# TensorE's block loop of a mixture of experts: 16 blocks a turn in place of four

## The reference

```python
T = x.shape[0]
scores = jax.nn.sigmoid(x @ gate_w)
...
_, selected_experts = jax.lax.top_k(masked_scores, K)
...
g = jax.lax.ragged_dot(xs, w_gate, group_sizes)
u = jax.lax.ragged_dot(xs, w_up, group_sizes)
d = jax.lax.ragged_dot(jax.nn.silu(g) * u, w_down, group_sizes)
...
expert_out = jnp.sum(out * weights[..., None], axis=1)
```

## Time and profile before

| what | us |
| --- | --- |
| median of 3 runs (lowest, highest) | 2470.41 (2468.43, 2471.7) |
| the profiled execution | 2471.61 |
| its span, first to last instruction | 2469.9 |
| PE busy | 2253.3 (91%) |
| PEld busy | 1931.8 (78%) |
| POOL busy | 1444.7 (58%) |
| DVE busy | 1266.8 (51%) |
| ACT busy | 1165.3 (47%) |

### The profile page before, as it was taken

One profiled execution on the slowest core, in us unless ns is written; L12 is line 12 of the kernel. 1 busy time (PEld: TensorE's weight loads), 2 busy tenths in 40 slices (PEclk: granted clock), 3 DMA queues, 4 the chain that ended last, 5 costly groups with the idle time before them and its releaser, 6 DMA issues. The chain is left out here.

```text
span 2469.9 us, 42008 instructions
## 1 busy us (share of the span) xinstructions
PE 2253.3 (91%) x12059; PEld 1931.8 (78%) x12060; DVE 1266.8 (51%) x2118; ACT 1165.3 (47%) x2503; POOL 1444.7 (58%) x980
## 2 busy tenths in 40 slices
PE   2899999999999999898989899999999799999776
PEld 1678888888888877776778699999988699999654
DVE  8767777777766656758643322222222122222365
ACT  4467777777777767776621123333332133333210
POOL 7877777777755558566713144441579956430376
PEclk9999999999999999999979999999999899999988
DMA  4533444443354456453357144442557655442476
GB/s 116 162 95 111 123 129 158 149 129 120 119 184 143 132 179 200 142 172 108 130 204 283 46 138 158 137 156 88 170 171 228 195 170 182 149 168 76 122 206 183
DMA packets 285670, 372.37 MB, mean 151 GB/s; under 512 B 20212, under 2 KB 187192, under 8 KB 280824
## 3 DMA queue, kind: packets, MB, share of 16 engines
q1 hardware_dynamic: 231224, 252.46, 32.7%
q10 hardware_dynamic: 38976, 68.17, 8.4%
q0 software_dynamic: 15360, 50.34, 6.2%
HBM read 257.66 MB, written 113.25 MB: 150 GB/s over the span
## 5 line engine op out<-in xcount | busy, mean ns | idle before, releaser
L1925 POOL TENSOR_SCALAR we_high<-we_raw 128x1408 fp32r<-128x1408 f32 (+1 forms) x95 | 134.0, 1410 | 396.5 <-PE up_e L650 315.9
L1927 POOL TENSOR_TENSOR we_low<-we_raw,we_high 128x1408 fp32r<-128x1408 f32 (+1 forms) x95 | 314.5, 3311 | 7.9
L2056 DVE TENSOR_TENSOR hT_low<-hT_ps,hT_high 128x256 fp32r<-128x256 f32 x127 | 54.0, 425 | 391.5 <-ACT hT_high L2019 391.5
L2069 DVE TENSOR_TENSOR hidden_e<-silu_e,up_e 128x352 f32<-128x352 f32 x127 | 66.2, 521 | 283.5 <-ACT silu_e L2030 283.5
L2030 ACT ACTIVATE silu_e<-gate_e 128x352 f32<-128x352 f32 x127 | 59.0, 465 | 316.7 <-PE up_e L650 316.7
L650 PE MATMUL gate_e<-we_high,xT_high 128*128 x508 | 177.7, 350 | 20.8 <-POOL we_low L1927 20.4
L2035 ACT ACTIVATE rows_out<-down_e 128x512 f32<-128x512 f32 x127 | 75.9, 598 | 215.5 <-PE down_e L650 215.5
L650 PE MATMUL gate_e<-we_high,xT_low 128*128 x508 | 166.0, 327 | 0.0
L650 PE MATMUL gate_e<-we_low,xT_high 128*128 x508 | 165.7, 326 | 0.0
L650 PE MATMUL up_e<-we_high,xT_high 128*128 x508 | 164.4, 324 | 0.0
L650 PE MATMUL up_e<-we_low,xT_high 128*128 x508 | 163.1, 321 | 0.0
(11 more groups left out here) (341 smaller groups left out, 7341.8 us busy)
## 6 DMA issues: line engine op xcount, KB each, us to landing
rows_early<-slots_in ACTq DMA_DIRECT2D x129, 256.0 KB, 2.7
slots_out<-rows_out ACTq DMA_DIRECT2D x127, 256.0 KB, 2.0
we_raw<-L_ffn_w_gate SPq DMA_DIRECT2D x32, 704.0 KB, 4.4
we_raw<-L_ffn_w_up SPq DMA_DIRECT2D x32, 704.0 KB, 5.0
w_ring<-L_attn_Wq SPq DMA_DIRECT2D x64, 256.0 KB, 3.2
q_T<-q_out SPq DMA_DIRECT2D x64, 256.0 KB, 2.5
w_ring<-L_attn_Wk SPq DMA_DIRECT2D x64, 256.0 KB, 3.5
w_ring<-L_attn_Wv SPq DMA_DIRECT2D x64, 256.0 KB, 3.9
```

The lines of the kernel that those rows point to most:

```text
L1925: nc.gpsimd.tensor_scalar(wh[:, p, at:to], raw[:, at:to], 1.0, 1.0, ALU.mult, ALU.mult).then_inc(w_hi, 1)
L1927: nc.gpsimd.tensor_tensor(wl[:, p, at:to], raw[:, at:to], wh[:, p, at:to].bitcast(F32), ALU.subtract).then_inc(w_split, 1)
L2069: nc.vector.tensor_tensor(hb[:], sg[:], psu[:], ALU.mult).then_inc(h_done, 1)
```

## The change

One argument differs: TensorE's loop holds 16 steps. By `pipeline`, steps 0 to 15 are written out, steps 16 to 111 are six turns of the loop, and steps 112 to 128 (17 of them) are written out. The other four engines' streams have the same instructions in the same order.

```diff
-            pipeline(pe, NBLK, 4, 2, step)
+            pipeline(pe, NBLK, 16, 2, step)
```

## The result

The changed kernel is slower. Its median of 4 runs is 2492.24 us (2490.94 to 2495.31), against 2469.52 of the kernel before in the runs beside it (2468.43 to 2471.70): a ratio of 1.0093, with 1.0075 to 1.0110 as its 95% interval. Forecast were 2478.1 with 2460 to 2487 as the range, so the sign of the likeliest case was right and the time lies outside the range. The profiled execution took 2493.31, which is 14.0 more than the 2479.3 forecast for it.

What follows compares the result with a forecast made beforehand. TensorE's steps were taken as the bound, with the sequencer's branch and late even steps on top, except where GpSimd bounds. Returns costing 16.4 less 8.7 saved gave 7.7 us longer: 2478.1 us, range 2460 to 2487.

Steps and rivals of the forecast that it cites:

- the likeliest case: TensorE's loop code comes back by packets at each return, so the kernel is 7.7 us longer; chance 0.68.
- the mechanism and the places: The loop's nine pages are not held; the array idles 2 to 4 us ahead of steps 32, 48, 64, 80, 96.
- The written-out stretches: Steps 3 to 15 and 112 to 123, written out at 6.67 us each, save 1.9 and 1.3 us.
- the one behind 63: The return behind step 63 costs 4.1 us, swallowed by TensorE's wait for GpSimd of 7.26 us.
- the wait at 1931: TensorE's wait for `we_low`, 7.26 us before, grows if the steps ahead of it get shorter.
- the price of a return, 4.1 us: At the loop's branch back: 2.65 us of idle array plus slow clock, 4.1; four returns count, 16.4 us.
- The upper end in the text: Highest cost of the loop's returns: 4 x (4.4 + 1.7), about 24 us.
- The fetch, 2.4 us: Bringing back a page of code at a return takes 2.4 us, between data landings of 2.0 and 2.7.
- The clock, 1.7 us: Behind a return the array's clock is at 0.50 for 3.4 us, costing half of that, 1.7.
- 6.77 for an even step inside the turn: Even steps in TensorE's loop take 6.77 us, not 6.67, since ScalarE's branch makes `hT_high` late.
- the saving of 5.5 us: Removed branches save 0.34 us each: 3.1 us in steps 16 to 60, 2.4 in steps 78 to 111.
- The first rival: The loop's nine pages are held and the whole 8.7 us gain shows: 2461.7 us; chance 0.26.

Runs made afterwards that it cites:

- 16 and 18 steps behind 8: Against the kernel before, TensorE's loop holds 16 or 18 steps after 8 written-out steps, over eight or nine pages: 1.0095 and 1.0096.
- 14 steps behind 14: Against the kernel before, TensorE's loop holds 14 steps after 14 written-out steps, 1727 instructions over eight pages: 1.0163, 2509.87 us.
- the four kernels with the reads together: Loops over seven pages long, all four reads of `tab` left at the step's head: changed kernel 1.0093, others against the kernel before 1.0095, 1.0096, 1.0163.
- 14 behind 8: Against the kernel before, TensorE's loop holds 14 steps after 8 written-out steps, 1726 instructions over seven pages: 0.9983, 2465.72 us.
- The straight kernel: Against the kernel before, all 129 steps of TensorE written out, no loop: 0.9950, 2478.45 us.
- the two kernels with the reads apart: Down's two reads of `tab` moved directly ahead of down's waits, in the kernel before and in the changed kernel: 0.9960 and 1.0047 against the kernel before.

## Why the prediction was wrong

**Right: the mechanism and the places.** Nine pages aren't held, the array stands ahead of steps 32, 48, 64, 80 and 96 and elsewhere only where it waits for GpSimd (idle times under 0.9 us left out), and the clock falls to 0.50 behind each. The written-out stretches gained what was worked out: -1.9 and -1.2 against -1.9 and -1.3. Four returns count and the one behind 63 is swallowed: steps 61 to 77 take 143.50 against 144.04, and the wait for `we_low` shrank from 7.26 to 4.70:

```profile
1938.21 0.65 PE L650 MATMUL gate_e<-we_high,xT_high 128*128 x1 [4.70 <-POOL we_low L1927]
```

The return cost 6.7 us by the same reckoning, the wait gave up 2.6, and most of the rest came from short waits for GpSimd ahead of it. There were four of 0.65 to 0.71 us before, 2.8 together, such as this one in PE's timeline of the kernel before; the changed kernel has none of them:

```profile
1859.98 0.42 PE L650 MATMUL gate_e<-we_high,xT_high 128*128 x1 [0.70 <-POOL we_low L1927]
```

One line of the prediction has the wait at 1931 grow since the steps before got shorter. It shrank, as its own step on the return behind 63 implies; the two lines didn't agree.

**Wrong: the price of a return, 4.1 us.** It is the term of 4 x 4.1 = 16.4 us. The step across the return and the one behind it, less the 7.11 and 6.71 that they took before, give 7.55, 6.58, 6.27 and 7.28 for the four that count: 27.7 us, 6.9 each. 11.3 of the 14.0 us are here. The upper end in the text, 4.4 + 1.7 = 6.1, didn't hold it either. Three things were short in it; of the 11.3 the fetch made 8.2, the clock 2.1 and the rest 1.0.

- *The fetch, 2.4 us.* I took it between two landings of data. The branch of the changed kernel takes 5.7, 4.2, 3.9 and 4.8 at the four returns, less the 0.215 of a held one 17.8 us, where 4 x 2.4 = 9.6 stood in the sum. In the return at 1732.7 (DMA of two windows: in 1732.7 to 1734.3 there is no q8 packet, in 1734.3 to 1736 there is one)

```profile
q8 instruction: 1, 0.02, 3.5%
```

  the packet begins at 1734.45 by its own record, 1.7 us after the branch, 3.5% of 1.7 us on 16 engines are 0.95 us, and the branch ends at 1736.9, 1.5 us after the packet. So 1.7 + 0.95 + 1.5 = 4.2, of which the transfer, which I had as the lower bound, is the smallest part. Over all 28 returns of the five kernels that fetch at them, the last part is nearly the same, 1.3 to 1.5 us from the packet's end to the branch's, the packet takes 0.9 to 1.7, and what differs most is how long it takes to begin, 0.9 to 3.7 us; why, the traces don't tell. The nearest rows for "issue to landing" lack that last 1.5 us. The value that would have fitted was in the earlier trace rows as well, 4.4, kept as the end.
- *The clock, 1.7 us.* The 3.4 us at 0.50 came from an idle time of 3.14. Here the array idles 4.0 to 5.9 us and the clock stays low for 6.80 behind all four. PE in these four windows, in the order of the returns behind 31, 47, 79 and 95:

```profile
1621.80:1628.60 6.80, 3.20 (x12) 0.50 0.72 244
1737.90:1744.70 6.80, 4.08 (x16) 0.50 0.53 158
1990.50:1997.30 6.80, 5.36 (x21) 0.50 0.19 52
2106.50:2113.30 6.80, 5.25 (x20) 0.50 0.17 47
```

  Half of the busy time is the cost: 1.6, 2.0, 2.7 and 2.6, together 8.9 where 6.8 stood in the sum.
- *A second wait, in one return.* The head of the loop lies at 0.86 of its page, not 0.77 (nine pages by either), and in the first return the next page isn't there when the sequencer reaches it. Two instructions of the sequencer, the last of the old page and the first of the new one, are 1.4 us apart there, where it is 0.4 to 0.6 us at the others:

```profile
L1980 PEldq ALU_OP  x1: 36/36/36, 1625.5 to 1625.5; - x1
```

```profile
L1982 PEldq EVENT_SEMAPHORE  x1: 51/51/51, 1626.9 to 1626.9; - x1
```

  It explains little: in that return 0.5 us are left beside the branch and the clock, and as much is left behind 47, where no such wait stands.

  Kernels with the head early in its page (16 and 18 steps behind 8) paid about 6.0 us on the mean for a counted return, those with the head at 0.86 and 0.93 (the changed kernel, and 14 steps behind 14) 6.9 to 7.0. The head's place isn't shown to be the reason, for the stretch at the low clock differs as well. In six of the ten counted returns with an early head it was 3.4 us and not 6.8, as here in the kernel with 18 steps, behind 25 and 97:

```profile
1602.85:1606.25 3.40, 3.40 (x15) 0.50 0.25 73
2145.57:2148.97 3.40, 3.40 (x15) 0.50 0.03 5
```

  Over the 20 counted returns of the four kernels with the reads together, those with 3.4 us at 0.50 cost 5.0 to 6.0, those with 6.8 cost 6.3 to 7.7, and the one with 10.2 cost 9.6. Branch less 0.215, plus half of the busy time at 0.50, gives the cost of 19 of them within 0.6 us; in the 20th, the 9.6, 1.6 us are left over, and there the second wait is seen, 1.7 us. Why the clock stays low for one length or another these traces don't tell: after idle times of 3.9 to 4.6 us both lengths occur.

That the way back fetches every page anew fits with 50 packets, ten a turn, where the text had eight per turn ("some 40"). Only the first one or two are waited for; the rest come while the array works, as in the written-out code.

**Wrong: 6.77 for an even step inside the turn.** It takes 6.86. The transposes of steps 39, 40 and 41 in the changed kernel's timeline of PE:

```profile
1674.50 0.52 PE L1969 MATMUL hT_ps<-ident,hidden_e 128*128 128x128 f32 x3
...
1681.20 0.49 PE L1969 MATMUL hT_ps<-ident,hidden_e 128*128 128x128 f32 x3
...
1687.98 0.52 PE L1969 MATMUL hT_ps<-ident,hidden_e 128*128 128x128 f32 x3
```

These are 6.70 and 6.78; over all steps inside the turns the median is 6.86 for even and 6.70 for odd ones. The 36 even steps of the two stretches that aren't behind a return are 3.4 us longer for it than 6.77 each; with the odd ones that is the saving of 5.5 us that came out as 1.9. Split on the sequencer, medians of the even steps inside turns: where the loop is held (before, 8 steps, 14 behind 8) down's issue takes 0.81 us and the four reads behind it 2.75, and from the end of L1992's wait to the next transposes it is 3.73; in loops that were fetched anew these are 0.84, 2.77 to 2.80, and 3.79 to 3.82. So 0.06 to 0.1 us is added per even step, and it shows in every loop of over seven pages with the four reads together (6.83 to 6.87) and in none of seven or fewer (6.77). What makes it I didn't find: the packets are there in time, the array is at full clock. The straight kernel, whose code is fetched too, issues down in 0.84 us in its even steps as well, so that part needs no return; its reads take 0.25 us less, which leaves slack, and its steps don't show it. It stays open. That the path itself is the sequencer's reads is shown by the two kernels with the reads apart, where even steps take 6.67.

**The sum.** 11.3 (returns) + 3.6 (even steps) - 0.5 (GpSimd's stretch) - 0.4 (ahead and behind) = 14.0, the whole miss.

**The first rival**, nine pages held, fell on the pages alone. Its other half stands: with the code held a longer turn is a gain, 0.17% for 14 steps in seven pages and 0.19% for eight steps in four, where 8.7 us (0.35%) were worked out for 16 steps.

The Trainium skill (Runtime: NRT & Kernel Launch, Instruction fetch mechanics) has two figures that these runs can now be held against. Its size of 128 KiB, eight pages, fits: seven pages of loop are held and eight aren't, if one of the eight goes to the page asked for ahead; the size itself no run measures. Its rule that a taken branch whose target is outside a window of two pages forces a fetch doesn't: the loop over seven pages returned seven times without a packet, in 0.215 us.

## What to carry to other kernels

Before a loop of TensorE is made longer, count the pages of 256 instructions that it touches from its own head, not its instructions: in this kernel seven stayed, and an eighth cost 5 to 8 us, twice 9 to 10, at each return where TensorE is the bound. The q8 line of the page tells at once which it is, and a straight stream is better than a loop that doesn't fit. And ask first what makes the branch dear: here it was the row of register reads that stood behind it on the sequencer, and moving two of them gave more than the longer loops that were held (0.40% against 0.17 and 0.19). It gave about as much as no loop at all (0.50%, and the intervals overlap).

## What was not expected of the hardware

- A return of the sequencer to a page that has left takes 3.5 to 6.1 us over the five kernels that had such returns. The packet starts 0.9 to 3.7 us after the branch, its transfer takes 0.9 to 1.7, and the sequencer goes on 1.3 to 1.5 us after it.
- A loop that is one page too long loses every page and not one: 9 packets a return for eight pages, 10 for nine.
- The same 14 steps, moved by 6 steps in the code, ran 0.9983 and 1.0163 of the time before.
- With refetched code an even step of the loop took 0.06 to 0.1 us longer, outside the returns; the cause is open.
- The clock stood at 0.50 for 3.4, 6.8 or 10.2 us behind a return, and this went with much of what one return cost more than another.
